# A graph layer with attention mix and experts on one core: router logits split between the node stage and the mix's second part, one deviation for two norms

## The reference, cut to what matters

```python
xn = layernorm(x)
state = x + gnn(xn) + mix(xn)
#   gnn = xn + z_in[in_deg] + z_out[out_deg] + sigmoid(cent @ W_cent + b_cent)
#            + sigmoid(vor @ W_vor + b_vor) + segment_sum(edge_attr @ W_sum + b_sum, src)
xs = layernorm(state)                       # the first norm of the node stage
out = state + experts(xs)
#   experts: logits = xs @ Wr + br; the two best of softmax(logits), weighted;
#            xt = (xs - mean(xs)) / sqrt(var(xs) + eps)     # the second norm
#            each expert: gelu((xt * g + b) @ W1 + b1) @ W2 + b2
```

## Time and profile before

| | us |
|---|---|
| median of 3 runs | 2354.43 (2350.54 to 2369.11) |
| the profiled execution | 2361.64 |
| its span | 2359.9 |
| edge stage, until the last scatter-add has landed | to about 1542 |
| node stage, first load of the tables to the first operation of routing | 1542.77 to 1649.62 |

### The profile page before, as it was taken

How to read it: one execution, slowest core, us unless ns; L and a number is a source line. 1 busy time by engine, 2 the same in 40 slices (tenths; PEclk the granted TensorE clock), 3 DMA queues, 4 the chain that set the end, 5 groups by cost and what they waited for, 6 DMA issues and landing times.

```text
span 2359.9 us, 38011 instructions
## 1 busy us (share of the span) xinstructions
PE 1735.6 (74%) x12869; PEld 1383.5 (59%) x12869; DVE 1451.0 (61%) x3795; ACT 727.5 (31%) x1607; POOL 1545.0 (65%) x1009
## 2 busy tenths in 40 slices
PE   2655544477777777677777777179589999999997
PEld 1333333345454544466566665178478888888886
DVE  2789977778778875233333333069866666666664
ACT  1011111144444444211111111047344433334432
POOL 2888888888888888888888888810034444545442
PEclk9676655579999999688888888589699999999999
DMA  9987777765555444555555554365538888878885
GB/s 301 234 181 172 146 154 151 145 103 75 70 69 75 69 69 69 81 74 78 74 85 79 73 85 65 37 167 168 185 98 271 252 252 244 271 240 259 254 268 157
DMA packets 401454, 348.00 MB, mean 147 GB/s; under 512 B 39304, under 2 KB 323531, under 8 KB 401261
## 3 DMA queue, kind: packets, MB, share of 16 engines
q1 hardware_dynamic: 268492, 266.72, 35.7%
q0 software_dynamic: 132768, 78.84, 28.6%
HBM read 236.69 MB, written 108.76 MB: 146 GB/s over the span
## 4 chain that ended last, share of the span: by engine, by line
PE 27%; DMA 26%; POOL 26%; issue 11%; DVE 7%; SPq 2%; ACT 0%; POOLq 0%; DVEq 0%; ACTq 0%
POOL node_table L1535 25%; DMA node_table<-edge_sums,row_i 19%; PE bank L730 10%; PE bank L744 8%; DMA big<-w_parts 6%; PE bank L687 2%; DVE hotB L871 2%; PE bank L699 1%; PE bank L701 1%; PE bank L522 1%; PE bank L679 1%; DVE hotA L868 1%; SPq L1584 1%; PE bank L716 1%; PE bank L482 1%
## 5 line engine op out<-in xcount | busy, mean ns | idle before, releaser
L1535 POOL DMA_INDIRECT node_table<-edge_sums,row_i x782 | 1256.2, 1606 | 278.9 <-issue 206.4
L482 PE MATMUL bank<-edge_rows,same_node 128*128 128x129 f32 x1564 | 293.0, 336 | 209.3 <-ACT edge_sums L1333 109.0
L1333 ACT COPY edge_sums<-bank 128x387 f32<-128x387 f32 (+1 forms) x261 | 125.0, 479 | 1044.1 <-DMA node_table<-edge_sums,row_i 749.6
L482 PEld LDWEIGHTS bank<-edge_rows,same_node 128*128 128x128 f32 x1564 | 250.5, 238 | 256.8 <-issue 228.1
L1561 POOL DMA_INDIRECT result<-mixw,edge_rows x105 | 167.6, 1596 | 307.1 <-DVE mixw L1290 150.1
L1487 ACT ACTIVATE mixw<-bank,edge_rows 128x256 f32<-128x256 f32 (+1 forms) x456 | 242.7, 550 | 354.9 <-PE bank L730 244.4
L730 PE MATMUL bank<-edge_rows,big 128*128 128x256 f16 (+1 forms) x2736 | 296.9, 269 | 21.6 <-DMA big<-w_parts 20.7
L730 PEld LDWEIGHTS bank<-edge_rows,big 128*128 128x128 f16 x2736 | 251.8, 99 | 61.6 <-DMA big<-w_parts 26.3
L744 PE MATMUL bank<-big 128*128 128x256 f16 x2520 | 284.4, 273 | 1.0 <-issue 1.0
L504 PE MATMUL bank<-hotA,hotB 128*128 128x49 bf16 x1564 | 116.9, 200 | 203.4 <-DVE hotB L871 202.2
L1550 POOL DMA_INDIRECT state<-xn_rows,edge_rows x105 | 116.3, 1107 | 221.5 <-DVE edge_rows L1249 189.8
(11 more groups left out here) (283 smaller groups left out, 2516.9 us busy)
## 6 DMA issues: line engine op xcount, KB each, us to landing
big<-w_parts SPq DMA_DIRECT2D x114, 1024.0 KB, 7.1
edge_rows<-edge_attr SPq DMA_DIRECT2D x130, 384.0 KB, 3.7
big<-L_ffn_W SPq DMA_DIRECT2D x128, 128.0 KB
w_parts<-big SPq DMA_DIRECT2D x64, 256.0 KB, 3.5
node_table<-z_parts SPq DMA_DIRECT2D x20, 640.0 KB, 7.4
node_table<-edge_sums,row_i POOLq DMA_INDIRECT x782
mixw<-node_table SPq DMA_DIRECT2D x96, 128.0 KB, 2.4
edge_rows<-L_ffn_b SPq DMA_DIRECT2D x57, 128.0 KB, 8.1
```

Source lines behind the costliest of these rows:

```text
L482: ins = e.matmul(ps_sum[:, i * XW:(i + 1) * XW], S[:, g % SRING, i * P:(i + 1) * P], X[:, c // LOAD % XRING, c % LOAD, :], start=True, sto ...
L1535: e.indirect_dma_start(table[t], bass.IndirectOffsetOnAxis(ap=row_i[:, g % ORING, i:i + 1], axis=0), O[:, g % ORING, i, 0:RW], None, compu ...
```

## The change

The logits of the router are linear in the state before its norm: with Wr' = Wr less the mean of its rows over the 256 features, the logits are r1 * (state @ Wr'), r1 being one over the deviation. state is the part known before the node stage plus the sum of the edges times W_sum. So the change

- subtracts Wr's mean (lin steps at v = 0 to 3 of the rest), multiplies W_sum by Wr' and puts these 8 columns behind W_sum's 256 (YW = 264); the projection then gives 264 columns, and state gets 8 more columns a tile (row_logit) to which VectorE adds them;
- computes the rest of the logits in the rest's steps: transposes of state at step 6, ScalarE's copy at step 7, the product with Wr' at step 8 (stages added to the schedule, which grows by four steps), one copy of all of them behind the last tile; ps_rest has three banks in place of four;
- takes both norms by one deviation: the second is sqrt((1+eps) var + eps^2), from the same variance; roots, reciprocal and -mean*r2 are taken for four tiles at once (STAT = 4), on ticks t+8 and t+9 of the group's last tile;
- lets ScalarE make hi and y (now already the twice normalised row) straight from state, with scale and bias (tick t+13), and VectorE lo = y - hi (tick t+14); the node stage has 64 ticks;
- multiplies the logits by r1 at the start of routing.

```diff
+STAT = 4
+STATS = -(-TILES // STAT)
+YW = DIM + EXPERTS
...
-REST_TICKS = (TILES - 1) * REST_EVERY + 6
+REST_TICKS = (TILES - 1) * REST_EVERY + 10
...
+def stat_of(t):
+
+    return t // STAT, slice(t // STAT * STAT, min(TILES, t // STAT * STAT + STAT))
...
-    PR, YR, HR = 8, 5, 3
+    PR, YR, HR = 8, 3, 3
...
     def tensor_rest(e, u):
         v = u - REST0
+        if v == 0:
+            e.wait_ge(deg_kept, 1)
+            for k in range(KC):
+                e.transpose(ps_turn[:, k * P:(k + 1) * P], wsum[:, k * P:(k + 1) * P], ident)
+            for k in range(KC):
+                ins = e.matmul(ps_turn[:, DIM:DIM + EXPERTS], ones, wr_t[:, k, :], start=(k == 0), stop=(k == KC - 1))
+            ins.then_inc(lin_pe, 1)
...
+        if (t := at_stage(v, 8, REST_EVERY, TILES)) is not None:
+            e.wait_ge(st_kept, t + 1)
+            for k in range(KC):
+                ins = e.matmul(ps_log[:, t * EXPERTS:(t + 1) * EXPERTS], stT[:, t % 2, k * P:(k + 1) * P], wr_t[:, k, :],
+                               start=(k == 0), stop=(k == KC - 1))
+            ins.then_inc(st_logit, 1)
+        if (t := at_stage(v, 6, REST_EVERY, TILES)) is not None:
+            if t == 0:
+                e.wait_ge(lin_dve, KC + 1)
+            else:
+                e.wait_ge(st_kept, t)
+            e.wait_ge(rest_added, 2 * t + 2)
+            for k in range(KC):
+                ins = e.transpose(ps_turn[:, k * P:(k + 1) * P], state[:, t, k * P:(k + 1) * P], ident)
+            ins.then_inc(st_turned, 1)
...
     def tensor_nodes(e, tick):
-        t = tick - 12
-        if 0 <= t < TILES:
-            e.wait_ge(n_yT, t + 1)
-            for k in range(KC):
-                ins = e.matmul(ps_log[:, t * EXPERTS:(t + 1) * EXPERTS], yT[:, t % 2, k * P:(k + 1) * P],
-                               wr_t[:, k, :], start=(k == 0), stop=(k == KC - 1))
-            ins.then_inc(n_logit, 1)
-        t = tick - 10
...
-            e.matmul(ps_s[t % 2][:, 0:DIM], sumT[:, t % 2, :], wsum, start=True, stop=True).then_inc(n_proj, 1)
+            e.matmul(ps_s[t % 2][:, 0:YW], sumT[:, t % 2, :], wsum, start=True, stop=True).then_inc(n_proj, 1)
...
     def vector_rest(e, u):
...
+        if at_stage(v, 9, REST_EVERY, TILES) == TILES - 1:
+            e.wait_ge(st_logit, TILES)
+            e.tensor_copy(row_logit, ps_log[:, 0:N8].rearrange("p (t e) -> p t e", e=EXPERTS)).then_inc(rest_added, 1)
...
     def vector_nodes(e, tick):
-        t = tick - 13
+        t = tick - 14
         if 0 <= t < TILES:
             e.wait_ge(n_hi, t + 1)
-            e.scalar_tensor_tensor(xh[:, t % HR, 1, :], y[:, t % YR, :], r2[:, t:t + 1], xh[:, t % HR, 0, :],
-                                   ALU.mult, ALU.subtract).then_inc(n_lo, 1)
+            e.wait_ge(n_y, t + 1)
+            if t >= HR:
+                e.wait_ge(xn_store[t % HR], 16 * (t // HR))
+            e.tensor_tensor(xh[:, t % HR, 1, :], y[:, t % YR, :], xh[:, t % HR, 0, :], ALU.subtract).then_inc(n_lo, 1)
...
-            e.tensor_scalar(y[:, t % YR, :], state[:, t, :], mv2[:, t, 0:1], r1[:, t:t + 1],
-                            ALU.subtract, ALU.mult).then_inc(n_y, 1)
-            e.tensor_scalar(r2[:, t:t + 1], r1[:, t:t + 1], r1[:, t:t + 1], mv2[:, t, 1:2], ALU.mult, ALU.mult).then_inc(n_y, 1)
...
+        t = tick - 9
+        if 0 <= t < TILES and t + 1 == stat_of(t)[1].stop:
+            g, w = stat_of(t)
+            e.wait_ge(n_sd, 2 * g + 2)
+            e.reciprocal(r12[:, :, w], r12[:, :, w]).then_inc(n_rstd, 1)
+            e.wait_ge(n_rstd, 2 * g + 1)
+            e.scalar_tensor_tensor(less[:, w], mv2[:, w, 0], -1.0, r12[:, 1, w], ALU.mult, ALU.mult).then_inc(n_rstd, 1)
...
     def vector_route(e):
-        then(e.tensor_tensor(logit, ps_log[:, 0:N8].rearrange("p (t e) -> p t e", e=EXPERTS), over_tiles(br_t), ALU.add))
+        then(e.tensor_tensor(logit, row_logit, b8(r1), ALU.mult))
+        then(e.tensor_tensor(logit, logit, over_tiles(br_t), ALU.add))
...
     def scalar_rest(e, u):
...
+        if (t := at_stage(v, 7, REST_EVERY, TILES)) is not None:
+            e.wait_ge(st_turned, t + 1)
+            if t >= 2:
+                e.wait_ge(st_logit, t - 1)
+            e.copy(stT[:, t % 2, :], ps_turn[:, 0:DIM]).then_inc(st_kept, 1)
...
     def scalar_nodes(e, tick):
-        t = tick - 12
+        t = tick - (STAT + 9)
         if 0 <= t < TILES:
-            e.wait_ge(n_r2, t + 1)
+            if t == stat_of(t)[1].start:
+                e.wait_ge(n_rstd, 2 * stat_of(t)[0] + 2)
             if t >= HR:
                 e.wait_ge(xn_store[t % HR], 16 * (t // HR))
-            e.activation(xh[:, t % HR, 0, :], y[:, t % YR, :], ACT.Copy, scale=r2[:, t:t + 1]).then_inc(n_hi, 1)
...
+                e.wait_ge(n_lo, t - HR + 1)
+            e.activation(xh[:, t % HR, 0, :], state[:, t, :], ACT.Identity, bias=less[:, t:t + 1], scale=r12[:, 1, t:t + 1]).then_inc(n_hi, 1)
+            e.activation(y[:, t % YR, :], state[:, t, :], ACT.Identity, bias=less[:, t:t + 1], scale=r12[:, 1, t:t + 1]).then_inc(n_y, 1)
...
-            e.activation(r1[:, t:t + 1], mv2[:, t, 1:2], ACT.Sqrt, bias=eps_t).then_inc(n_sd, 1)
+            e.activation(r12[:, 0, w], mv2[:, w, 1], ACT.Sqrt, bias=eps_t).then_inc(n_sd, 1)
+            e.activation(r12[:, 1, w], mv2[:, w, 1], ACT.Sqrt, bias=eps_s, scale=(1.0 + EPS) * XSCALE ** -2).then_inc(n_sd, 1)
...
     def sync_nodes(e, tick):
-        t = tick - 13
+        t = tick - 14
...
-                e.wait_ge(rest_added, 2 * TILES)
+                e.wait_ge(rest_added, 2 * TILES + 1)
```

More of the change, by code:

```diff
@@ L166, in build_layer @@
     mixw = sb("mixw", [P, 8192])
-    state = sb("state", [P, TILES, DIM])
+    rows = sb("state", [P, TILES, YW])
+    state, row_logit = rows[:, :, 0:DIM], rows[:, :, DIM:YW]
     src_i = big[:, 5000:5000 + ETILES].bitcast(I32)
@@ L303, in build_layer @@
     y = part(YR * DIM).rearrange("p (r n) -> p r n", r=YR)
-    yT = part(2 * DIM).rearrange("p (r n) -> p r n", r=2)
     xh = part(HR * DIM).bitcast(F16).rearrange("p (r i n) -> p r i n", r=HR, i=2)
     mv2 = late(2 * TILES).rearrange("p (t i) -> p t i", i=2)
-    r1, r2 = late(TILES), late(TILES)
-    ps_t, ps_s, ps_y, ps_log = banks[0:2], banks[2:4], banks[5:7], banks[7]
+    r12, less = late(2 * TILES).rearrange("p (i t) -> p i t", i=2), late(TILES)
+    r1 = r12[:, 0, :]
+    ps_t, ps_s = banks[0:2], banks[2:4]
     at[0] = 0
@@ L358, in build_layer @@
     XG = 8
-    xg = state.rearrange("p t n -> p (t n)")[:, 0:XG * 2 * DIM].bitcast(F16).rearrange(
+    xg = rows.rearrange("p t n -> p (t n)")[:, 0:XG * 2 * DIM].bitcast(F16).rearrange(
         "p (r s i k n) -> p r s i k n", r=XG, s=2, i=2, k=KC)
@@ L758, in tensor_program @@
                 tensor_rest(e, u)
-        for tick in range(TILES + 13):
+        for tick in range(TILES + 15):
             tensor_nodes(e, tick)
@@ L1127, in vector_nodes @@
         if 0 <= t < TILES:
[L1128 removed]
+            if t == 0:
+                e.wait_ge(rest_added, 2 * TILES + 1)
+            st = rows[:, t, :]
             e.wait_ge(n_proj, t + 1)
[L1130 to L1139 removed]
+            e.tensor_tensor(st, st, ps_s[t % 2][:, 0:YW], ALU.add).then_inc(n_state, 1)
         t = tick - 7
```

85 lines of the change are left out of this document (37 added, 48 removed).

## The result

The changed kernel takes 2353.04 us in the median of 22 runs, the kernel before 2360.77 us in as many; the ratio is 0.9969, 95% interval 0.9957 to 0.9981, so 7.3 us less (4.5 to 10.2). The three runs that the forecast started from had a median 6 us under that of the 22. The forecast was 12.9 us less: the right sign and the right place, too large a gain.

The account below looks back on a forecast made before the run. TensorE bounds the node stage before, the ring of three row buffers after. Stage -13.5 us, routing +0.6, net -12.9: 2361.64 becomes 2348.7 profiled, and 2341.5 us as the runs' median, 7 us lower; range 2331 to 2357.

Parts of the forecast that it names:

- The edge stage hides the moved work: Edge stage: 30 us of TensorE and 18 us of ScalarE work added, 0 us expected; rival without cover 2371.5 us, chance 0.04.
- VectorE, ScalarE: Node stage: VectorE about 1.3 us a tile, at most 1.4; ScalarE 1.4, not over 1.5; Identity 0.60 us.
- The bound moves to the ring of three, with the stores behind SP's loads: Node stage: hi waits for the store three tiles back, with y in the cycle; 6.40 us for four tiles.
- The start of the sum: Head of node stage: projection 2 starts at 1553.79 us as before, then nine at 1.34 us until 1565.9.
- 34 tiles at 1.60 us: Node stage from about projection 11, paced by the ring of row buffers: 54.4 us, until 1620.3 us.
- SP's floor of 1.40: SP's queue in the node stage: four loads and two stores for two tiles, 2.78 us, 1.39 a tile.
- The rival in which SP or TensorE is the floor: Node stage: ring hidden, 1.40 or 1.34 us a tile, 2334.7 or 2332.5 us in all; chance 0.27.
- The tail: End of node stage: ScalarE's last hi, eight at 1.25 us, plus 1.6 us; 11.6 us, routing at 1636.1.
- The median: Whole kernel: the runs' median lies 7 us below the profiled execution, so 2348.7 us becomes 2341.5 us.
- Landings grow under load: Rival, node stage: store landings reach 4.1 us, 2.05 us a tile, 2356.8 us in all; chance 0.08.
- TensorE's clock: Rival, node stage: TensorE stays at 1.2 GHz, 2.64 us a tile, 2380.6 us in all; chance 0.04.

Follow-up runs that it names:

- e1: The kernel before plus only the work moved into the edge stage, its results unused and the node stage as before: ratio to before 0.9995.
- e4: The changed kernel without ScalarE's y, the low half being taken from state (other values): ratio to before 0.9937, node stage 91.7 us.
- e2: The changed kernel with rings of six in place of three for row halves and y: ratio to before 0.9938, node stage 91.4 us.
- e11: The kernel before with a ring of six row halves in place of three, nothing else: ratio to before 1.0000, node stage 105.2 us.
- e5: The changed kernel with rings of six for row halves and y, and row stores issued by GpSimd: ratio to before 0.9919, node stage 84.2 us.
- e3: The changed kernel with table loads split two and two over even and odd ticks, ring of three: ratio to before 0.9964, node stage 94.4 us.
- e7: The changed kernel, rings of three kept, with row stores issued by GpSimd in place of SP: ratio to before 1.0022, node stage 106.6 us.
- e10: The changed kernel with rings of six, row stores by GpSimd, statistics for two tiles and earlier hi, lo and store: ratio to before 0.9930, stage 82.5 us.
- e12: The changed kernel with rings of six, table loads issued by GpSimd and stores by SP: ratio to before 0.9933, node stage 87.2 us.
- e6: The kernel before with only the logits moved out of the node stage, norms still tile by tile: ratio to before 0.9986, node stage 100.2 us.
- e9: The changed kernel with statistics tile by tile, lo and store one tick behind hi: ratio to before 0.9963, node stage 96.3 us.

## Why the prediction was right and where it was wrong

- *The edge stage hides the moved work*: right, at 0 us (e1, whose interval leaves room for 2.1 us), and the first load of the tables starts at 1542.8 us in both first profiles.
- *VectorE, ScalarE*: right as to their being under the bound (VectorE busy 13.5 to 14.4 of 20 us, ScalarE 14.4 to 14.6). ScalarE's Identity took 0.60 and 0.59 us, as priced.
- *The bound moves to the ring of three, with the stores behind SP's loads*: right. Hi waits for stores, y stands in the cycle (e4), six in place of three frees it (e2), and the same edit does nothing to the kernel before (e11).
- *The start of the sum*: projection 2 came at 1552.9 for 1553.8, as TensorE's clock had risen before the first projection; 1 us of luck, which hides a part of the next term.
- *34 tiles at 1.60 us*: this is the term that failed. From projection 11 (1564.9) to 45 (1623.9) they took 59.0 us for 54.4, 1.74 a tile. The cycle itself came nearly as priced: four tiles without a long issue take 6.4 to 6.8 us for 6.40. What I left out is SP's long issues. They stood in the trace of before, where the longest issue of 100 was 1.849 us beside a median of 0.469, and I took the median alone:

```profile
L1769 SPq DMA_DIRECT2D mixw<-node_table x100: 359/469/1849, 1542.8 to 1632.6; - x100
```

  In the changed kernel three of the 17 pairs have one, of 1.47, 1.54 and 2.16 us: 3.8 us over the median, 0.11 a tile of the 0.14 that were missing. In e2, where SP has no pause, the three long ones (1.93, 1.58 and 1.36) are 3.5 us over it. The last projection came at 1627.9 for 1624.5.
- *SP's floor of 1.40*: wrong too, 1.53 (e2), as a store takes 0.43 to 0.47 us when issued without a pause, and 0.33 behind one. The rival in which SP or TensorE is the floor, at 1.34 to 1.40, could not have been reached by way of SP.
- *The tail*: 11.6 us forecast from the last projection to routing, 10.9 measured (10.6 in the table, which counts from the projection's second record); it gave 0.7 us back. Routing began at 1638.8 for 1636.1, so the stage gave 10.8 us for 13.5, net of routing's extra product 10.2 for 12.9.
- *The median*: of the 11.5 us between the forecast's 2341.5 and 2353.0, 6.3 are the start. That the median lies 7 us under the profiled execution was taken from three runs (2354.4); of 22 it is 2360.8, 0.9 us under it. 2.7 us are the stage. The other 2.5 are a gain that the stage shows and the medians don't (7.3 by the ratio, with 10.2 at the interval's end). No run shows where they go; e1's interval would allow for 2.1 of them in the edge stage.
- *Landings grow under load*: in the changed kernel the median landing of a store is 2.2 us at a DMA share of 0.74, before it was 2.4 at 0.68 (1565 to 1615), so this rival did not come. The rule of the Trainium skill, "DMA: Bandwidth & Descriptors", section "Latency and other measured facts", gives an HBM access 0.2 us on average and 2 us at high load. The trace does not agree at this load. At higher ones it goes that way: SP's stores take 2.6 us in e2, at 0.81, and its loads 3.2 us in e5, at 0.93, where they took 2.4 in the changed kernel. But the stores of e3 take 3.0 at 0.74, so the share alone does not say it.
- *TensorE's clock*: 0.91 to 1.00 in the stage, with TensorE busy 83 to 91%. It fell once, to 0.50 from 1594.5 to 1597.9 us, after the pause that a long issue had left; the transposed sum of a tile took 1.81 us for 1.05 and ScalarE waited 1.2 us for it. But the store for which ScalarE's next hi had to wait landed at 1598.1 and this hi started at 1598.34, so the fall cost 0.2 us at most.

## What to carry to other kernels

When an engine at 100% is relieved, look at once for the shortest ring that closes through a DMA: its period is (operations + what stands before the store in its queue + landing) over the tiles that it spans, and an operation put between its two ends, here y, counts in full. Count a queue's issues per tile with their mean, long ones included, and not their median. A ring's depth is free to try while memory is there, but it is worth something only when the engine that hid it has been relieved. And when a step is moved to another queue, look at what its wait had held back in the old one: in e5, e7 and e10 it was store_y.

## What the hardware showed that was not expected

- An issue on SP takes 0.47 us for 128 KB and 0.04 us pass before the next; in the changed kernel four of 149 take 1.4 to 2.2 us, and in every run where SP issues the loads one to four are over 1 us. What makes one long was not found out. It is not SP's issuing alone: the stores issued just before the three long ones (at 1568.06, 1588.57 and 1609.69) land after 3.2, 3.6 and 3.8 us, where the median of all is 2.1. In e12, where GpSimd issues the loads, none of SP's 49 stores takes over 0.36 us and none of the loads over 0.81.
- GpSimd issues the plain store in 0.54 us and the load in 0.72. Its stores land after 2.9 us in the median (e7) and 3.5 (e5), its loads after 3.7 (e12), SP's stores after 2.2 to 2.6 in the changed kernel and e2, but after 3.0 in e3 and 3.9 in e12, so it is not the issuing queue alone that sets the landing.
- The node stage's DMAs moved 290 GB/s at a share of 0.93 (e5), so 204 before was no limit.
- The medians of e5, e7, e10 and e12, in which GpSimd issues plain DMAs, gain 4 to 8 us less than their stages. But the changed kernel, e3 and e6, without such DMAs, gain 3 to 4 us less too, and e1, e2, e4, e9 and e11 at most 2. The intervals reach 3 to 6 us to either side, so whether any of it belongs to GpSimd's DMAs stays open.
